# A convolution and a top-2 mixture of experts on one core: every chunk routed alone, one region per expert, expert tiles in two rounds

## What is computed

```python
x = x + relu(conv3x3(layernorm(x), kernel, groups=8) + bias)
t = x.reshape(4096, 128)
n = layernorm(t)
logits = n @ router_w.T                       # 8 experts
vals, idx = top_k(logits, 2)
w = softmax(vals)
y_e = (silu(n @ w_gate[e]) * (n @ w_up[e])) @ w_down[e]      # hidden width 256
out = t + sum_k w[:, k] * y_{idx[:, k]}
```

## Time and profile before

| | |
|---|---|
| runs (3) | 277.93, 278.57, 279.11 us |
| profiled execution, first to last instruction | 277.2 us |
| mean granted TensorE clock of that execution | 0.866 of full |
| POOL busy | 163.6 us (59%), 78 result scatters and 64 token scatters |
| PE busy | 202.9 us (73%) |
| DVE, ACT busy | 140.8 us (51%), 119.0 us (43%) |
| first and last gate/up matmul of the experts | 109.5 and 253.4 us |

### The profile page before, as it was taken

How to read it: one execution, slowest core, us unless ns; L and a number is a source line. 1 busy time by engine, 2 the same in 40 slices (tenths; PEclk the granted TensorE clock), 3 DMA queues, 4 the chain that set the end, 5 groups by cost and what they waited for, 6 DMA issues and landing times.

```text
span 277.2 us, 4518 instructions
## 1 busy us (share of the span) xinstructions
PE 202.9 (73%) x1186; PEld 174.3 (63%) x1186; DVE 140.8 (51%) x457; ACT 119.0 (43%) x285; POOL 163.6 (59%) x184
## 2 busy tenths in 40 slices
PE   6699576975529595739998654993999999999000
PEld 5687464864428484428887544883898789898000
DVE  3557696555241724445755322451458866555025
ACT  2369544745902353073453322342445454454100
POOL 5644388743775277725777777764356576666600
PEclk9599895999957777757999999898899999999855
DMA  7993010100133351100232232343239523361075
GB/s 235 380 381 116 0 48 30 53 29 10 48 94 82 78 115 59 48 10 31 74 87 70 68 78 78 100 134 84 61 68 303 159 72 96 99 195 43 15 237 217
DMA packets 26648, 28.99 MB, mean 105 GB/s; under 512 B 4957, under 2 KB 18409, under 8 KB 26624
## 3 DMA queue, kind: packets, MB, share of 16 engines
q1 hardware_dynamic: 21776, 20.03, 25.1%
q0 software_dynamic: 4544, 8.47, 9.1%
q10 hardware_dynamic: 304, 0.20, 0.2%
HBM read 16.93 MB, written 12.67 MB: 107 GB/s over the span
## 4 chain that ended last, share of the span: by engine, by line
PE 28%; POOL 21%; issue 13%; DVE 12%; DMA 11%; SPq 6%; ACT 6%; POOLq 1%; ACTq 0%; DVEq 0%
POOL zs L992 11%; POOL yb L1005 9%; PE ps_gu L349 7%; PE ps_y L439 5%; DMA yb<-y,zt 3%; PE ps_gu L419 3%; PE ps_gu L421 3%; PE ps_gu L420 3%; PE ps_h L429 3%; SPq L303 3%; DMA zt<-zs 3%; ACT zr L547 2%; DMA spare<-yb 2%; PE ps_z L408 2%; DVE bn L637 2%
## 5 line engine op out<-in xcount | busy, mean ns | idle before, releaser
L1005 POOL DMA_INDIRECT yb<-y,zt x78 | 76.3, 978 | 40.0 <-ACT y L583 24.6
L992 POOL DMA_INDIRECT zs<-zr,slot x64 | 63.0, 984 | 38.0 <-issue 18.3
L349 PE MATMUL ps_gu<-pad,ckw 128*128 128x256 f32 x192 | 53.7, 439 | 0.0
L349 PEld LDWEIGHTS ps_gu<-pad,ckw 128*128 128x128 f32 x192 | 41.7, 224 | 7.1
L842 DVE TENSOR_TENSOR hh<-ps_gu,sg 128x512 f32<-128x512 f32 (+1 forms) x40 | 27.1, 678 | 35.7 <-ACT sg L574 35.7
L439 PE MATMUL ps_y<-wall,hT 128*128 x312 | 41.9, 278 | 0.0
L439 PEld LDWEIGHTS ps_y<-wall,hT 128*128 128x128 f32 x312 | 38.7, 195 | 0.1
L574 ACT ACTIVATE sg<-ps_gu 128x512 f32<-128x512 f32 (+1 forms) x40 | 23.5, 586 | 33.3 <-PE ps_gu L421 33.3
L583 ACT ACTIVATE y<-ps_y,zt 128x128 f32<-128x128 f32 x78 | 24.4, 365 | 30.1 <-PE ps_y L439 30.1
L419 PE MATMUL ps_gu<-wall,z_lo 128*128 x78 | 36.4, 467 | 0.0
L408 PE MATMUL ps_z<-ident,zt 128*128 128x128 f32 x78 | 17.1, 302 | 21.2 <-DMA zt<-zs 15.2
(11 more groups left out here) (131 smaller groups left out, 225.9 us busy)
## 6 DMA issues: line engine op xcount, KB each, us to landing
zt<-zs SPq DMA_DIRECT2D x78, 65.0 KB, 2.0
spare<-yb SPq DMA_DIRECT2D x16, 256.0 KB, 4.5
xt<-x_rows SPq DMA_DIRECT2D x8, 256.0 KB, 5.3
xc<-x_cols SPq DMA_DIRECT2D x8, 256.0 KB, 6.6
spare<-gate_up_w SPq DMA_DIRECT2D x8, 256.0 KB, 6.3
out<-xt SPq DMA_DIRECT2D x8, 256.0 KB, 3.0
yb<-y,zt POOLq DMA_INDIRECT x78, 2.3
zs<-nulls SPq DMA_DIRECT2D x18, 65.0 KB, 3.3
```

The lines of the kernel that those rows point to most:

```text
L349: last = nc.tensor.matmul(dst, ckw[:, h * BANDS + k, :], pad[n % 2][:, h * IMG:(h + 1) * IMG, below:below + PAIRS, dx:dx + WW], start=k == ...
L992: nc.gpsimd.indirect_dma_start(zs[g], bass.IndirectOffsetOnAxis(slot[:, k, n * TT + t:n * TT + t + 1], 0), zr[n % ZR][:, t, k, :], None, b ...
L1005: nc.gpsimd.indirect_dma_start(yb, bass.IndirectOffsetOnAxis(zt[:, u % RING, s, P:P + 1].bitcast(U32), 0), y[u % YB][:, s, :], None, bound ...
```

## The change

- **Routing by chunk.** Every chunk is a batch of its own. Logits come out of the same matmul as the transposed rows (identity and router weights side by side, `ident_x`), ACT copies them to SBUF, and `top_two` uses the DVE's MAX and MAX_INDEX, four of each per chunk, in place of ten dependent steps.
- **POOL only scatters** after its constants. The power moves away: ACT takes a square root (`deviation_x`, `deviation_t`), DVE a reciprocal and a Newton step (`inverse_x`, `inverse_t`, five dependent small instructions). Ids are written once at the start. The weights leave the scattered rows (`ROW` is 129, not 130) and are applied in `add_rows`.
- **One region per expert**, for all 8 chunks, in one table `zs`. `zr` has a buffer for every chunk.
- **Tiles in two rounds.** Round 1 holds 24 tiles (12 units) that are full after 4 chunks; `first_table` makes its list. Round 2 holds the other tiles, padded to 47 (24 units), in an order by the chunk that completes them; `second_table` makes that list, in the expert stage behind `gated(2)`. The sum is 71 tiles and 36 units, not 78 and 40. SP loads round 2 once all scatters of chunks 4 to 7 have landed.
- **Rings.** `zt` holds 18 units, the results `y` 16 units (they use the memory of the loaded weights).
- **The end.** Results are read back, added and stored chunk by chunk, chunks 4 to 7 as their units are done. The read-back goes to `zr`, in pieces of 512 bytes. `add_rows` is 8 instructions per chunk (multiply by the weight and add), and those of chunks 0 to 3 stand behind the last four steps of the expert pipeline.
- The alternation on POOL stays as it was: 2 token scatters of chunks 6 and 7, 2 result scatters.

The diff, cut to its core:

```diff
-BATCHES = [(0, 1), (1, 2), (2, 4), (4, 6), (6, 8)]
-SETS = [(0, 3), (3, 5)]
-TILES = [2 * nt + E - 1 for nt in NT]
+EARLY = CHUNKS // 2
+CAP = TOK + P
+NULL = E * CAP
+TILES1 = EARLY * N * 2 // P - E
+TILES2 = (CHUNKS - EARLY) * N * 2 // P + 2 * E - 1
...
-RING = 8
-YB = 8
-ZR = 4
+RING = 18
+YB = 16
...
+            sp.wait_ge(table_ready, 1)
+            for n in range(EARLY):
+                sp.wait_ge(scattered[n], 16 * 2 * TT)
+            for u in range(0, FIRST[1], 4):
+                load_units(u, min(u + 4, FIRST[1]))
+            pad_regions()
+            for n in range(EARLY, CHUNKS):
+                sp.wait_ge(scattered[n], 16 * 2 * TT)
+            sp.wait_ge(nulls_stored, 16 * (E + 1))
+            sp.wait_ge(table_ready, 2)
+            for u in range(FIRST[1], GATHER_AFTER, 4):
+                load_units(u, min(u + 4, GATHER_AFTER))
+            await_results(EARLY - 1)
+            for n in range(EARLY):
+                gather_rows(n)
+            for u in range(GATHER_AFTER, UNITS, 4):
+                load_units(u, min(u + 4, UNITS))
+            await_results(EARLY)
+            gather_rows(EARLY)
+            for n in range(EARLY):
+                store_rows(n)
+            for n in range(EARLY + 1, CHUNKS):
+                await_results(n)
+                gather_rows(n)
+                store_rows(n - 1)
+            store_rows(CHUNKS - 1)
...
+            def inverse_t(n):
+                nc.vector.reciprocal(guess2[:, i], sd2[:, i]).then_inc(dev2_step, 1)
+                nc.vector.scalar_tensor_tensor(off2[:, i], mv2[:, i, 1], EPS_FFN, guess2[:, i], ALU.add, ALU.mult
+                nc.vector.scalar_tensor_tensor(half2[:, i], off2[:, i], -0.5, guess2[:, i], ALU.mult, ALU.mult
+                nc.vector.scalar_tensor_tensor(rstd2[:, i], half2[:, i], 1.5, guess2[:, i], ALU.add, ALU.mult
+                nc.vector.scalar_tensor_tensor(nmr2[:, i], mv2[:, i, 0], -1.0, rstd2[:, i], ALU.mult, ALU.mult
...
+            def add_rows(n):
+                for k in range(2):
+                    for t in range(TT):
+                        i = n * TT + t
+                        last = nc.vector.scalar_tensor_tensor(xt[:, i, :], zr[n][:, t, k, 0:P], share[:, k, i:i + 1],
+                                                              xt[:, i, :], ALU.mult, ALU.add)
...
+            for n in range(1, CHUNKS + 1):
+                if n >= 3:
+                    slots(n - 2)
+                residual(n - 1)
+                if n in (2, 4):
+                    inverse_x(n // 2 + 2)
+                if n >= 3:
+                    inverse_t(n - 2)
+                top_two(n - 1)
+                stats_t(n - 1)
+                if n + 1 < CHUNKS:
+                    pad_odds(n + 1)
...
+                if 3 <= n <= 7:
+                    weight_tails((1, 3, 5, 6, 7)[n - 3])
+                if n == EARLY + 1:
+                    first_table()
+                if n == EARLY + 2:
+                    table_row(0)
```

More of the change, by code:

```diff
@@ L131, in metaformer_moe @@
[L131 to L132 removed]
+        logits = sb("logits", [P, CHUNKS * TT, E])
+        top8 = sb("top8", [P, CHUNKS * TT, E])
+        which8 = sb("which8", [P, TT, E], U32)
+        oh = sb("oh", [P, 2, TT, E])
+        mask = sb("mask", [P, TT + 1, E], BF16)
+        base = sb("base", [P, CHUNKS, E])
+        place = sb("place", [P, TT, E])
+        chosen = sb("chosen", [P, 2, TT, E])
@@ L276, in load_units @@
-                i = 2 * (first - FIRST[g])
+                r = ROUND_OF_UNIT[first]
+                i = 2 * (first - FIRST[r])
                 held = sum(COUNT[first:last])
                 _, rows = nc.values_load_multi_w_load_instructions(
-                    tab[g][0:1, TILES[g] + i:TILES[g] + i + held], engines=[mybir.EngineType.SP],
-                    min_val=0, max_val=E * CAP[g],
-                    skip_runtime_bounds_check_because="the table's rows are clamped to the null tile on the chip")
+                    tab[r][0:1, ROUNDS[r] + i:ROUNDS[r] + i + held], engines=[mybir.EngineType.SP],
+                    min_val=0, max_val=NULL,
+                    skip_runtime_bounds_check_because="the table's rows lie in the regions or are the null tile")
```

932 lines of the change are left out of this document (434 added, 498 removed).

## The result

Four runs of the changed kernel took 262.19, 264.06, 264.91 and 265.89 us, median 264.49, against 278.25 of the kernel before on the same chip: a ratio of 0.951 (95% interval 0.945 to 0.957). It is faster. The prediction, 262.6 us (253 to 274) with 0.87 for faster, holds. The profiled execution is the one of 262.19 us; its span is 260.4 us, and in all four runs the time is 1.8 us above the span. The profiled execution of before, with a span of 277.2, was by the same 1.8 one of about 279.0 (an estimate), 0.8 above its median.

The account below looks back on a forecast made before the run. No engine bounds the whole span, so five stretches were summed: -7.3 + 1.0 - 22.4 + 13.2 - 0.5 = -16.0, span 277.2 to 261.2, with 1.4 for the median 262.6 us; range 253 to 274.

Parts of the forecast that it names:

- Stretch 3: From the last token scatter to PE's restart: 7.2 us against 29.6, -22.4.
- Stretch 4: From PE's restart to the last gate/up's end, bound by PE: 49 tiles, 73.5 us against 60.3, +13.2.
- Stretch 2: POOL's alternation, first result scatter to last token scatter: same steps, second table on DVE delays the second unit, +1.0.
- ACT's table load: Second table load on ACT, for the square root, before silu(0): hidden beside gate/up of unit 0, 0 us.
- Stretch 1: Start to first result scatter: a series over DVE and ACT sets the pace; scatter at 121.7 instead of 128.98, -7.3.
- The five passes: Stage 1 from residual 2 at 41.3 to residual 7 at 98.7: 57.4 us in all.
- Stretch 5: From PE's end to the last instruction, a chain over SP's reads and stores: 23.3 us against 23.8, -0.5.
- the rival of the longer end: Slower 512-byte read-back landings, SP in steps with DVE, and a second table stalling POOL: 269 us; chance 0.12.
- Routing on DVE: Rival: MAX or MAX_INDEX on DVE bounds stage 1; gain gone at 0.25 more than 0.1 each; slower, chance 0.07.
- Overlaps better: Rival: stage 1's ACT relu and copies run in DVE's shadow, a pass of 9.6, time 255 us; chance 0.14.
- The rounds did what they say: Rival denied here: SP queues for something else before round 2; 285 us if the old 29.6 stayed; chance 0.02.
- some 17 us between chunk 6's first pair and the first result scatter: POOL's idle time there, listed as a sign that the prediction is right.

Follow-up runs that it names:

- Experiment 7: Changed kernel with SP writing the null rows only after the last token scatter has landed, as in the kernel before: 272.37 us.
- experiment 3: Changed kernel with the tile ring back at 8 units instead of 18: 268.00 us.
- Experiment 2: Changed kernel with 20 tiles in round 1 instead of 24, and 51 in round 2 instead of 47: 270.25 us.
- Experiment 10: Changed kernel with the second table moved on DVE from step 2 to step 5 of the expert pipeline: 261.96 us.
- Experiments 5 and 12: inverse_t without its Newton step: in the changed kernel 259.58 us; in the best combined version, itself 236.30 us, 231.59 us.
- experiment 4: Changed kernel with SP issuing the read-backs of chunks 5 to 7 before the stores of chunks 0 to 6: 258.49 us.
- experiment 6: Changed kernel with read-backs of chunks 4 to 7 in 2 KB pieces to a contiguous buffer, not 512 bytes to zr: 262.46 us.
- experiment 1: Changed kernel with all 64 token scatters issued on POOL before its first result scatter: 245.99 us.
- experiment 8: Changed kernel with token scatters first, reads before stores, all tile loads before the first read, additions of chunks 0 to 4 in halves: 240.95 us.

## Why the prediction was right, and where it was not

**Stretch 3, -22.4 (measured -22.6).** Right in size and in its two parts: landing 2.30 for 2.4, table read 1.83 and first load 1.87 with what lies between for 4.83. Experiment 7 gives 7.9 of it to the early null rows. The rest is SP's wait for ring places behind a first set of 20 units. The reason given, 12 units in a ring of 18, named two changes where one was enough: with the ring back at 8 the gap is the same (experiment 3). Whether the larger ring alone would do is open.

**Stretch 4, +13.2 (+13.9).** 49 tiles behind the gap; the units follow one another in 2.947 us as before. Experiment 2 confirms the rule with another number of tiles. Of the excess of 0.7, 0.5 lies in the restart, 2.0 us instead of 1.5 (its first unit took 5.5 us), the rest in the pitch.

**Stretch 2, +1.0 (+1.5).** The second table took 4.4 us on DVE (4.6 summed), and POOL lost 1.53. Experiment 10 removes just that.

**ACT's table load, 0.** It took 1.28 us at 106.58, and ACT then waited 0.89 more for PE before the first silu: hidden. By the Trainium skill (ScalarE: Activation LUTs, What ACT_TABLE_LOAD costs), a switch takes 2.66 us with its drain; from the start of the load to silu are only 2.17 here, and a matmul released it, so the page's figure is not reached and the measurement decides.

**Stretch 1, -7.3 (-12.8): mis-sized by 5.5.** The first residual came at 20.39 (0.6 earlier than taken). Two uneven passes took 20.0 (20.3). The five passes took 54.08 instead of 57.4, 0.66 less each: routing 1.53 instead of 1.8, `slots` 0.62 instead of 0.85, and 0.15 from instructions of DVE that follow one another closer than their lengths (0.60 from residual to the next, not 0.69; inverse 0.99, not 1.05). From the last residual to gate/up it took 11.3, as summed. From gate/up to the first result scatter 10.4 instead of 11.7. So of the 5.5 us the five passes make 3.3, and of these the routing 1.35, `slots` 1.15 and the closeness of DVE's instructions 0.75; the head up to the first residual and the uneven passes make 0.9, the way to the first result scatter 1.3. Experiments 5 and 12 show that the mechanism, one series, was right for most of it: what leaves the series leaves the time. It wasn't right for the pass from residual 5 to residual 6, where the path went over PE's slow convolution and DVE waited 4.87 us instead of 3.33; there the prediction had PE waiting in every pass. Part of the 12.8 is luck of the clock: in the traces of experiments 3, 7 and 10, with the same code up to there, the first result scatter came at 117.52, 118.91 and 119.04, not at 116.18. The forecast also had the whole gain behind the first gate/up; that gain is 9.1 (10.4 us from gate/up to the first result scatter, against 19.5), and 3.7 lie before it. No run put the old routing or the powers on POOL back, so how much of stage 1 each of them gives isn't shown.

**Stretch 5, -0.5 (+3.2): mis-sized by 3.7.** The chain was named right (SP reads chunk n only after storing chunk n-2), and experiment 4 shows it by cutting it. Two terms were too small. Eight additions take 2.32 us, not 1.85: they follow one another in 0.29, and the 0.21 that I took from BN_STATS wasn't the right neighbour. (I put that down to their two operands in SBUF, but no run shows it: on 512 columns the residual, with two operands in SBUF, and a copy out of PSUM take 0.68 each.) With a start 0.5 later than summed that is 1.2 until the read of chunk 5, and 0.5 for each of the chunks 5 and 7, 2.2 in all. And the reads: from the first issue to the landing 4.5 where I had 3.4 (chunk 5), and 4.2 where I had 3.5 (chunk 7), 1.8 in all, of which the pieces of 512 bytes make 1.5 (experiment 6). SP's step from the additions of chunk 5 to the next read added 0.1, and the way from the last addition to the end, 2.45 instead of 2.9, gave 0.45 back. This is the rival of the longer end, which I had put at 269; it came in full, but stretch 1 covered it.

**The rivals.** Routing on DVE didn't become dear: a MAX takes 0.09 and the pair of a MAX_INDEX 0.14, where 0.35 each would have undone the gain. "Overlaps better" had a pass of 9.6, with ACT's work in the shadow of DVE's; that didn't come, since DVE still waits 3.33 us for ACT in a pass; the passes were shorter for other reasons. The rounds did what they say. Two small things in the sums: the median of the change lies above its runs' spans by 1.8 us and not by 1.4, and the chances of a faster kernel add up to 0.88, not 0.87.

**What I did not see.** The prediction named POOL's idle time, "some 17 us between chunk 6's first pair and the first result scatter", as a sign of being right, and took it as given. The alternation behind it is the largest loss that an experiment found in the changed kernel: experiment 1 gives back 18.5 us.

## What to carry to other kernels

An engine that alternates two kinds of work in a written order waits for the later kind with the earlier one ready behind it. Look in its timeline for an idle stretch whose releaser belongs to one kind, and ask who waits for the other: here six token scatters stood ready behind a result scatter, and PE was idle for 15 us some 40 us later. The order costs more than the idle stretch itself, since every result scatter issued in between delays the last token scatter too. Count the work as well as the waits: in the expert stage seven tiles fewer gave some 10 us, and PE's idle time fell by only 3.6. A read ordered behind a store, or a long helper computation ahead of a short step in a pipeline, are the same mistake in a smaller size. When summing a series of short instructions, take the distance from start to start in a row of the same instruction at the same size, not a duration and not another instruction.

## What the runs showed of the hardware

**The first convolution at either clock.** Its 12 matmuls took 2.83 us in the change's profiled run, and 5.00 in that of experiment 7, which is the same code up to there. Windows of the two traces (busy us and instructions of PE, PEld, DVE, ACT, POOL, then granted clock, DMA share, GB/s):

```profile
13.00:20.00 7.00, 6.49 (x31) 5.39 (x32) 5.07 (x28) 5.57 (x13) 3.73 (x3) 1.00 1.05 387
```

```profile
13.00:20.00 7.00, 7.00 (x25) 5.78 (x26) 3.44 (x19) 4.14 (x9) 3.72 (x3) 0.69 1.05 386
```

With 1.00 the first residual starts at 20.39, with 0.69 at 22.38. The pass to residual 2 then takes 7.70 and 8.79 us, and the last residual starts at 94.49 and 97.37, 2.9 apart. Ahead of the first convolution PE had waited 2.06 and 1.85 us. The medians, -13.8, are therefore the better measure of the whole. The Trainium skill (TensorE: Matmul & The Clock Gate, Part 1: The HAM clock gate) says that the same kernel meets the slow clock for a different number of matmuls in different runs; the two traces agree, with 2 us for it here.

**PE after a wait.** At the restart of the change, after 15.09 us idle, gate/up matmuls follow one another in 0.43 us (160.48, 160.91, 161.34, 161.76) against 0.23 later; the granted clock is 0.51 from 159 to 165 us, the lower level, and 1.00 from 165 to 200. A short wait does it too: in the change and in experiment 1 PE waits 2.79 us ahead of the second unit's transposes, and behind it gate/up matmuls stand 0.43 apart (in experiment 1 at 124.25, 124.67 and 125.10) before they return to 0.24. At the place of the restart experiment 1, where PE doesn't stop, has nothing of the kind.

**Scatters beside additions.** Beside additions with two operands in SBUF some of POOL's scatters took 1.04 to 1.18 instead of 0.97, in the change and in experiment 8; others didn't (in the change the one of 239.98 took 0.97, that of 241.25 took 1.12, both beside the same row of additions). By the Trainium skill (SBUF — State Buffer, Who interferes with whom) the one that comes second stands still until the other's instruction ends. With additions that follow one another every 0.29 us, a scatter lost at most 0.21. That the port is the cause is not shown: no run changed the additions' operands.
